# One layer on one core: the copy of the transposed probabilities is issued in front of the mask-and-maximum of a step

## The chip, the cores and the metric

The program runs on one core of one Trainium2 chip. The metric is the device time of one launch in microseconds (us), the median of three runs. The engines are called as in the profile: PE is TensorE (matmul; PEld its weight loads), DVE is VectorE, ACT is ScalarE, POOL is GpSimd, SP is SyncE.

## The reference, cut to what matters

Sizes: B=4, L=1024, D=256, 16 heads of 16, windows of 64 tokens; 8 experts, 2 per token, hidden size 1024.

```python
xn = layernorm(x)                                   # over D
# attention: each block of 64 queries sees its own 64 keys and the 64 before it
scores = einsum('bhnqd,bhnkd->bhnqk', qb, k_kv) * 0.25
scores = where(band_mask, scores, -1e30)
attn = softmax(scores, axis=-1)
ob = einsum('bhnqk,bhnkd->bhnqd', attn, v_kv)
# mixture of experts: top 2 of 8 with a capacity, relu(disp @ w1 + b1) @ w2 + b2, weighted by the gate
out = x + (ob, heads joined) @ w_out + moe(xn)
```

## The kernel before, in words

Four phases follow one another, each a block of its own: the norm, the routing, the experts (`moe_phase`), and the attention (`attention_phase`, line 788), which ends with the residual, the gathered outputs of the experts and the store. The change lies in the attention phase, which takes the span from about 461 us on.

The attention phase cuts the 4096 tokens into 8 units of 512 tokens (two to a batch element). A unit is 16 steps (`STEPS`), so there are 128 steps; a step `t` is one head pair's share of four tiles (`BLK` = 4) of 128 queries-by-keys, that is a tile of 128x512. For a step the engines do, each in its own loop over steps and with its own lag:

- PE writes the scores of two steps at a time (line 1212, at every even step, for steps t+2 and t+3). Before it does, it waits for the mask-and-maximum of all steps up to `t` (line 1205), because the bank of PSUM that holds the scores of step t+2 is the one of step `t`.
- DVE adds the mask to the scores, scales, writes them to SBUF and takes the row maximum, four instructions to a step (line 1088, "mask-and-maximum"); each releases ACT.
- ACT takes the exponential and its row sum (line 1059), four to a step.
- DVE takes the reciprocal of the sums of two steps at once (line 1096), at every even step, for steps t-2 and t-1, and releases POOL.
- POOL multiplies the probabilities by it (line 990, four to a step), and at every even step issues one gather of the experts' outputs (line 1000).
- PE transposes the probabilities of step t-4 (line 1226) into one of two banks of PSUM, `psP`; it first waits for POOL and for the copy of step t-6, which held that bank.
- DVE copies the transposed probabilities of step t-5 from `psP` to `pT` in SBUF (line 1103, "copy").
- Every fourth step PE multiplies them with the values (line 1246), and ACT and DVE bring the result out (lines 1041, 1130, 1046, 1135).

Between these PE works off the projections of the next unit and the output product of the last one in parts (lines 1170 and 1185, `psA`), which ACT and DVE read out (DVE lines 1070, 1075 and 1142). At every odd step DVE also adds one gathered tile of the experts' outputs to the residual (line 1122).

The order is written out by hand: each engine runs its program in order, and the steps of one engine follow each other as its `steps` function lists them. In a step DVE's list is: mask-and-maximum, reciprocal (even steps), copy, read-outs of `psA`, gathered tile (odd steps), and, every fourth step each, lines 1130 and 1135. `alone` is a wait that is an instruction of its own.

```python
LAG_T, LAG_C, LAG_V, LAG_O = 4, 5, 6, 7
...
pe.wait_ge(max_done, (b * BS + t - 1) * BLK)             # scores(b, t): masks of all steps before t-1
...
pe.wait_ge(pT_done[g % 2], b * STEPS + g // 2)           # transpose g: copy g-2
```

Of the kernel before, what the change touches and what calls it, by code (L numbers as in the profile page):

```python
# [40 lines left out]
def alone(eng, sem, value):  # L41


    eng.wait_ge(sem, value)
    eng.sem_inc(Mem.passed, 1)
# [742 lines left out]
def attention_phase(nc, m, x, xn_dram, y_dram, out):  # L788
# [11 lines left out]
    STEPS = NH // 2 * UB // BLK  # L800
    UNITS = B * 2

    LAG_T, LAG_C, LAG_V, LAG_O = 4, 5, 6, 7
# [20 lines left out]
    PR, PTR, YG = 8, 8, 4  # L824
    GRP = 4
    ctx = ExitStack()
    with ctx:
# [16 lines left out]
        pT = sb("a_pT", [P, PTR, BLK, P], fp32)  # L844
# [9 lines left out]
        psP = [ps("a_psP0"), ps("a_psP1")]  # L854
# [8 lines left out]
        t_done, pT_done = two("a_t_done"), two("a_pT_done")  # L863
        pv_done = sem("a_pv_done")
# [9 lines left out]
        BS, HB = 2 * STEPS, NI  # L874

        def count(b, u, i, first, last):

            n = NI * u + PRO - UT + i
            if first and u == 0 and i < O_FIRST:
                n += UT  # L880
            if last and u == 1:
                n -= O_FIRST
            return b * HB + n // 2
# [8 lines left out]
        def ended(t, first, last):  # L892

            if t is None or t >= BS:
                return []
            return [(i,) + there(t, i, first, last) for i in done_at[t % STEPS] if there(t, i, first, last)]

        def batches(eng, body, tail):

            body(0, True, False)  # L900
            for b in range(1, B - 1):
                body(b, False, False)
            body(B - 1, False, True)
            tail(B - 1)

        def lagged(t, lag, first):

            return None if first and t < lag else t - lag

        def group_out():  # L910

            return psO[:, :].rearrange("p (n s t) -> p n s t", n=BLK, s=2)

        def o_cols(parts, g):

            i = g // GRP % (STEPS // GRP)
            cols = slice((i % 2) * BLK * WIN, (i % 2 + 1) * BLK * WIN)
            return parts[g // STEPS % 2][:, i // 2, cols].rearrange("p (n t) -> p n t", n=BLK)
# [146 lines left out]
        @block.vector  # L1065
        def _(dve):
            def read_item(kind, j, u, n, bank, xh_count):
                if kind == "x":
                    dve.wait_ge(x_high, xh_count)
                    dve.tensor_tensor(xTl[:, j, :], psA[bank][:, :], xTh[:, j, :].bitcast(fp32), ALU.subtract)\  # L1070
                        .then_inc(item_free[bank], 1)
                elif kind == "k":

                    dve.wait_ge(item_done[bank], n + 1)
                    dve.tensor_copy(kT[u][:, j, WIN:WIN + UL], psA[bank][:, :]).then_inc(item_free[bank], 1)

            def steps(b, ts, first, last):
                for t in ts:
                    if t < BS:
                        r = t % PR  # L1080
                        if not (first and t < PR):

                            dve.wait_ge(t_done[t % 2], b * STEPS + (t - PR) // 2 + 1)
                        alone(dve, s_done, b * BS + t + 1)
                        for j in range(BLK):

                            band = 1 if t < STEPS and t // GRP % 2 == 0 and j == 0 else 0
                            dve.tensor_tensor_reduce(  # L1088
                                out=pr[:, r, j, :], in0=psS[bank_of[t % 4]][:, j * P:(j + 1) * P],
                                in1=m.mask[:, band, :], scale=-(DH ** -0.5), scalar=BIG,  # L1090
                                op0=ALU.add, op1=ALU.min, accum_out=nmax[:, r, j:j + 1]).then_inc(max_done, 1)
                    g = lagged(t, 1, first)
                    if g is not None and g < BS and g % 2 == 1:
                        pair = slice((g - 1) % PR, (g - 1) % PR + 2)
                        dve.wait_ge(exp_done, (b * BS + g + 1) * BLK)
                        dve.reciprocal(rsum[:, pair, :], sums[:, pair, :]).then_inc(rsum_done, 2)  # L1096
                    g = lagged(t, LAG_C, first)
                    if g is not None and g < BS:
                        dve.wait_ge(t_done[g % 2], b * STEPS + g // 2 + 1)
                        if not (first and g < PTR):  # L1100

                            dve.wait_ge(pv_done, b * (BS // GRP) + (g - PTR) // GRP + 1)
                        dve.tensor_copy(pT[:, g % PTR, :, :].rearrange("p c q -> p (c q)"), psP[g % 2][:, :])\  # L1103
                            .then_inc(pT_done[g % 2], 1)
                    for i, u, kind, j in ended(lagged(t, LAG_I, first), first, last):
                        n = count(b, u, i, first, last)
                        if kind == "o":
                            add_out((1 - u) % 2, j, n, i % 2, (b * 2 + u) * K * UT)
                        else:
                            read_item(kind, j, (1 - u) % 2, n, i % 2, (b * 2 + u + 1) * KD + j + 1)  # L1110
                    g = lagged(t, LAG_Y, first)
                    if g is not None and g < BS and g % 2 == 0:
                        u, i = g // STEPS % 2, g % STEPS // 2
                        ub = b * 2 + g // STEPS
                        tile, k = i // K, i % K
                        if i == 0:
                            dve.wait_ge(res_in[u], 16 * (b + (g // STEPS + 2) // 2))

                        dve.wait_ge(yg_in[i % YG], 16 * (ub * (K * UT // YG) + i // YG + 1))
                        if k == 1:  # L1120
                            dve.wait_ge(acc, ub * K * UT + i)
                        dve.scalar_tensor_tensor(res[u][:, tile, :], yg[i % YG][:, :],  # L1122
                                                 m.gates[:, bass.ds(ub * UT + k * NT + tile, 1)],
                                                 res[u][:, tile, :], ALU.mult, ALU.add).then_inc(acc, 1)
                    g = lagged(t, LAG_O, first)
                    if g is not None and g < BS and g % GRP == GRP - 1:

                        r = g // GRP % 2
                        dve.wait_ge(o_even, b * (BS // GRP) + g // GRP + 1)
                        dve.scalar_tensor_tensor(of[:, r, :, :], group_out()[:, :, 1, :], parity[:, 1:2],  # L1130
                                                 of[:, r, :, :], ALU.mult, ALU.add).then_inc(o_free, 1)
                    g = lagged(t, LAG_O + 1, first)
                    if g is not None and g % GRP == GRP - 1:
                        dve.wait_ge(o_high, b * (BS // GRP) + g // GRP + 1)
                        dve.tensor_tensor(o_cols(oTl, g), of[:, g // GRP % 2, :, :], o_cols(oTh, g).bitcast(fp32),  # L1135
                                          ALU.subtract).then_inc(o_low, 1)

            def add_out(u, j, n, bank, sums_before):

                dve.wait_ge(acc, sums_before)  # L1140
                dve.wait_ge(item_done[bank], n + 1)
                dve.tensor_tensor(res[u][:, j, :], res[u][:, j, :], psA[bank][:, 0:D], ALU.add)\  # L1142
                    .then_inc(item_free[bank], 1)

            def tail(b):
                steps(b, range(BS, BS + LAG_O + 1), False, True)
                for j in range(UT):
                    add_out(1, j, count(b, 1, NI - UT + j, False, True), j % 2, UNITS * K * UT)
            batches(dve, lambda b, first, last: steps(b, range(BS), first, last), tail)

        @block.tensor
# [181 lines left out]
```

## Time and profile before

| | |
|---|---|
| median of 3 runs | 759.27 us (757.99 to 761.73) |
| the profiled execution's own time | 760.58 us |
| its span | 758.8 us |
| DVE, ACT, POOL busy in the span | 63%, 63%, 56% |
| PE, PE weight loads busy in the span | 93%, 80% |

The span is what the engines' first and last instruction enclose; 1.8 us of the execution's own time lie around it. The shares are averages over four phases with different limits; the attention phase has to be read by itself. In the rows below `L1088` is line 1088 of the kernel, `out<-in` are the names of the tiles, and a bracket behind an instruction gives the time that its engine sat idle before it and what ended that.

### The profile page before, as it was taken

To read this page: it belongs to the slowest core of one execution; us is meant where nothing else is said; L and a number is where in the kernel's file an instruction comes from. 1 tells how busy PE (TensorE), PEld (TensorE's weight loads), DVE (VectorE), ACT (ScalarE), POOL (GpSimd) and SP (SyncE) were. 2 spreads that over 40 slices of the span, in tenths; PEclk is the share of its full clock that TensorE was granted. 3 is DMA by queue.
4 is the path that set the end of the run, shared out by engine and by line. 5 is a ranking of instruction groups with operands and counts; after the bars stand their busy time and mean duration, and the time that the engine had idled before them with its cause. 6 is when DMAs were issued, how large, how long until landed. Compare 5 with 4: busy or idle time off the path is not lost. (4 is left out here: it accounts for less than half of the span.)

```text
span 758.8 us, 18403 instructions
## 1 busy us (share of the span) xinstructions
PE 705.8 (93%) x5816; PEld 603.4 (80%) x5817; DVE 481.7 (63%) x1774; ACT 480.2 (63%) x1508; POOL 427.7 (56%) x818
## 2 busy tenths in 40 slices
PE   6686799999999999999999997999999999999885
PEld 3364689898898988989889896788888878878664
DVE  7773243543425345253452524999999989999994
ACT  4640480834709357192561905998989989999891
POOL 4502560543605336153351303899999989999993
PEclk8875699999999999999999998999999999999897
DMA  9722231142311423123241013132333415141411
GB/s 314 277 77 77 87 104 58 62 138 83 110 56 60 140 76 114 54 74 125 76 124 42 0 43 108 35 91 85 96 96 85 121 53 141 37 120 36 115 57 42
DMA packets 52308, 69.95 MB, mean 92 GB/s; under 512 B 6672, under 2 KB 44816, under 8 KB 52240
## 3 DMA queue, kind: packets, MB, share of 16 engines
q1 hardware_dynamic: 45744, 52.31, 21.3%
q0 software_dynamic: 6144, 16.79, 8.0%
q8 instruction: 32, 0.52, 0.3%
q14 instruction: 36, 0.29, 0.1%
q10 hardware_dynamic: 352, 0.04, 0.0%
HBM read 47.75 MB, written 16.78 MB: 85 GB/s over the span
## 5 line engine op out<-in xcount | busy, mean ns | idle before, releaser
L1059 ACT ACTIVATE a_p<-a_p,a_nmax 128x128 f32<-128x128 f32 x512 | 198.6, 395 | 35.6 <-DVE a_nmax L1088 35.4
L990 POOL TENSOR_SCALAR a_p<-a_p,a_rsum 128x128 f32<-128x128 f32 x512 | 192.3, 391 | 18.8 <-DVE a_rsum L1096 16.5
L719 DVE TENSOR_TENSOR m_hl<-m_hf,m_hh 128x512 fp32r<-128x512 f32 x128 | 93.1, 727 | 100.3 <-ACT m_hh L676 100.3
L55 PE MATMUL m_psY<-m_w2h,m_hh 128*128 128x256 f32 x512 | 145.1, 283 | 0.0
L55 PE MATMUL m_psY<-m_w2l,m_hh 128*128 128x256 f32 x512 | 143.8, 281 | 0.0
L55 PE MATMUL m_psY<-m_w2h,m_hl 128*128 128x256 f32 x512 | 143.8, 281 | 0.0
L672 ACT ACTIVATE m_hf<-m_psF,b1T 128x512 f32<-128x512 f32 x128 | 88.4, 691 | 66.3 <-PE m_psF L55 52.1
L640 POOL CAST m_w2h<-raw 128x256 fp32r<-128x256 f32 x64 | 25.4, 396 | 175.8 <-PE m_psY L55 120.5
L1088 DVE CUSTOM_DVE_ANT_0 a_p<-a_psS,mask 128x128 f32<-128x128 f32 x512 | 116.6, 281 | 6.3 <-PE a_psS L1212 5.1
L55 PE MATMUL m_psF<-m_xh,w1h 128*128 128x512 f32 x256 | 103.6, 405 | 1.9 <-DVE m_xl L696 1.9
L55 PE MATMUL m_psF<-m_xh,w1l 128*128 128x512 f32 x256 | 102.1, 399 | 0.0
L55 PE MATMUL m_psF<-m_xl,w1h 128*128 128x512 f32 x256 | 102.0, 398 | 0.0
L1059 ACT ACTIVATION_READ_ACCUMULATOR a_p<-a_p,a_nmax 128x1 f32 x512 | 99.5, 194 | 0.0
L705 DVE TENSOR_TENSOR y<-m_psY,b2b 128x256 f32<-128x256 f32 x64 | 27.2, 425 | 113.2 <-PE m_psY L55 113.2
L55 PEld LDWEIGHTS m_psY<-m_w2l,m_hh 128*128 128x128 f32 x512 | 96.5, 189 | 0.4
L55 PEld LDWEIGHTS m_psY<-m_w2h,m_hh 128*128 128x128 f32 x512 | 96.4, 188 | 0.4
L55 PEld LDWEIGHTS m_psY<-m_w2h,m_hl 128*128 128x128 f32 x512 | 96.5, 188 | 0.0
L660 ACT ACTIVATE m_xh<-m_psT 128x512 fp32r<-128x512 f32 x32 | 19.1, 600 | 113.9 <-PE m_psT L741 98.9
L1226 PE MATMUL a_psP<-eye,a_p 128*128 128x128 f32 x512 | 83.9, 288 | 5.2 <-DVE a_pT L1103 4.0
L676 ACT ACTIVATE m_hh<-m_psF,b1T 128x512 fp32r<-128x512 f32 x128 | 87.2, 681 | 0.0
L1103 DVE COPY a_pT<-a_psP 128x512 f32<-128x512 f32 x128 | 84.6, 661 | 1.7 <-PE a_psP L1226 1.4
L1226 PEld LDWEIGHTS a_psP<-eye,a_p 128*128 128x128 f32 x512 | 58.6, 145 | 20.5 <-POOL a_p L990 7.7
(186 smaller groups left out, 1363.1 us busy)
## 6 DMA issues: line engine op xcount, KB each, us to landing
raw<-in_L_ffn_w SPq DMA_DIRECT2D x16, 1024.0 KB, 5.3
y_scratch<-y SPq DMA_DIRECT2D x64, 128.0 KB, 1.7
n_xin<-in_L_attn_x SPq DMA_DIRECT2D x8, 512.0 KB, 7.4
xn_scratch<-n_xn SPq DMA_DIRECT2D x8, 512.0 KB, 7.6
a_res<-in_L_attn_x SPq DMA_DIRECT2D x8, 512.0 KB, 3.8
out<-a_res SPq DMA_DIRECT2D x8, 512.0 KB, 3.0
xnr<-xn_scratch SPq DMA_DIRECT2D x7, 512.0 KB, 5.1
b2b<-in_L_ffn_b SPq DMA_DIRECT2D x8, 128.0 KB, 4.8
```

What stands on the lines that cost most here:

```text
L55: last = pe.matmul(out, a, b, start=(n_start and i == 0), stop=(n_stop and i == n - 1))
L640: pool.tensor_copy(w2h[:, c, :], raw2[:, c, :]).then_inc(w2h_done, 1)
L660: act.activation(xh[:, g % KD, (g // KD) * HALF:(g // KD + 1) * HALF], psT[g % 2][:, :], ACT.Copy)\
L672: act.activation(hf[:, u % FR, :], psF[u % 4][:, :], ACT.Relu, bias=bias)
L676: act.activation(hh[:, u // HC, u % HC, :], psF[u % 4][:, :], ACT.Relu, bias=bias)\
L705: dve.tensor_tensor(yb[:, s % YR:s % YR + 1, :], psY[s % 2][:, 0:D].unsqueeze(1), m.b2b[:, bass.ds(e, 1), :], ALU.add).then_inc(yb_done, 1)
L719: dve.tensor_tensor(hl[:, u // HC, u % HC, :], hf[:, u % FR, :], hh[:, u // HC, u % HC, :].bitcast(fp32), ALU.subtract).then_inc(hl_done, 1)
L990: pool.tensor_scalar(e, e, rsum[:, r, j:j + 1], 0.0, ALU.mult, ALU.add).then_inc(norm_done, 1)
L1059: act.activation(e, e, ACT.Exp, scale=-1.0, bias=nmax[:, r, j:j + 1], accum_out=sums[:, r, j:j + 1]).then_inc(exp_done, 1)
L1088: dve.tensor_tensor_reduce(out=pr[:, r, j, :], in0=psS[bank_of[t % 4]][:, j * P:(j + 1) * P], in1=m.mask[:, band, :], scale=-(DH ** -0.5), ...
L1103: dve.tensor_copy(pT[:, g % PTR, :, :].rearrange("p c q -> p (c q)"), psP[g % 2][:, :])\
L1226: ins = pe.transpose(psP[g % 2][:, j * P:(j + 1) * P], pr[:, g % PR, j, :], m.eye[:, :])
```

## The change

DVE's list for a step begins with the copy of step t-5; the mask-and-maximum and the reciprocal follow it. The copy's two waits (for the transpose, and for the product that used the slot of `pT` before) move with it. Nothing else is edited: the same instructions, the same tiles, the same lags.

```diff
             def steps(b, ts, first, last):
                 for t in ts:
+                    g = lagged(t, LAG_C, first)
+                    if g is not None and g < BS:
+                        dve.wait_ge(t_done[g % 2], b * STEPS + g // 2 + 1)
+                        if not (first and g < PTR):
+
+                            dve.wait_ge(pv_done, b * (BS // GRP) + (g - PTR) // GRP + 1)
+                        dve.tensor_copy(pT[:, g % PTR, :, :].rearrange("p c q -> p (c q)"), psP[g % 2][:, :])\
+                            .then_inc(pT_done[g % 2], 1)
                     if t < BS:
                         r = t % PR
...
                         dve.reciprocal(rsum[:, pair, :], sums[:, pair, :]).then_inc(rsum_done, 2)
-                    g = lagged(t, LAG_C, first)
-                    if g is not None and g < BS:
-                        dve.wait_ge(t_done[g % 2], b * STEPS + g // 2 + 1)
-                        if not (first and g < PTR):
-
-                            dve.wait_ge(pv_done, b * (BS // GRP) + (g - PTR) // GRP + 1)
-                        dve.tensor_copy(pT[:, g % PTR, :, :].rearrange("p c q -> p (c q)"), psP[g % 2][:, :])\
-                            .then_inc(pT_done[g % 2], 1)
                     for i, u, kind, j in ended(lagged(t, LAG_I, first), first, last):
```

## Rows read from the trace of the kernel before

**Rows 1.** The busy line of the page: us, share of the span, instructions.

```profile
PE 705.8 (93%) x5816; PEld 603.4 (80%) x5817; DVE 481.7 (63%) x1774; ACT 480.2 (63%) x1508; POOL 427.7 (56%) x818
```

**Rows 2.** Two units by window: length, busy us by engine, PEclk, DMA share, GB/s.

```profile
600.70:637.50 36.80, 35.64 (x402) 29.73 (x401) 34.62 (x177) 32.51 (x147) 32.51 (x74) 0.95 0.30 77
672.10:706.70 34.60, 34.13 (x402) 28.67 (x401) 34.47 (x178) 32.56 (x147) 32.26 (x74) 1.00 0.29 79
```

**Rows 3.** Waits in the attention phase: us in total, times, longest.

```profile
POOL a_p L990 <- DVE a_rsum L1096: 16.5, 25, 6.8
PEld a_psS L1212 <- DVE a_nmax L1088: 15.9, 26, 1.6
...
PE a_psP L1226 <- DVE a_pT L1103: 4.0, 4, 1.2
...
DVE a_rsum L1096 <- ACT a_p L1059: 1.0, 3, 0.5
```

**Rows 4.** The chain that ended last, 664 to 700 us, by line.

```profile
by line: PE a_psA L1185 29.0%; PE a_psS L1212 24.4%; PE a_psP L1226 20.3%; PE a_psO L1246 11.2%; DVE a_p L1088 5.5%; PE a_psA L1170 3.0%; issue 2.1%; DVE a_pT L1103 1.7%; DVE a_res L1142 0.9%; DVE a_res L1122 0.8%; DVE a_oTl L1135 0.4%; DVE
```

**Rows 5.** Groups of instructions: busy us, mean ns; the last: ns min/median/max.

```profile
L990 POOL TENSOR_SCALAR a_p<-a_p,a_rsum 128x128 f32<-128x128 f32 x512 | 192.3, 391 | 18.8 <-DVE a_rsum L1096 16.5
L1088 DVE CUSTOM_DVE_ANT_0 a_p<-a_psS,mask 128x128 f32<-128x128 f32 x512 | 116.6, 281 | 6.3 <-PE a_psS L1212 5.1 <-issue 1.2
...
L1103 DVE COPY a_pT<-a_psP 128x512 f32<-128x512 f32 x128 | 84.6, 661 | 1.7 <-PE a_psP L1226 1.4 <-issue 0.2
...
L1122 DVE SCALAR_TENSOR_TENSOR a_res<-a_yg,gates,a_res 128x256 f32<-128x256 f32 x64 | 37.0, 577 | 1.8 <-DMA a_yg<-y_scratch,a_idx 1.8
...
L1122 DVE SCALAR_TENSOR_TENSOR a_res<-a_yg,gates,a_res x64: 466/574/743, 474.7 to 746.8; 128x256 f32<-128x256 f32 x64
```

**Rows 6.** PE in order of time, one unit: start, length, instruction.

```profile
664.97 1.16 PE L1212 MATMUL a_psS<-a_k,a_q 32*128 32x128 f32 x16 [0.60 <-DVE a_nmax L1088]
...
688.06 0.66 PE L1226 MATMUL a_psP<-eye,a_p 128*128 128x128 f32 x4
...
699.57 1.16 PE L1212 MATMUL a_psS<-k,q 32*128 32x128 f32 x16 [0.47 <-DVE a_nmax L1088]
```

**Rows 7.** DVE in order of time, the same unit.

```profile
687.63 0.68 DVE L1103 COPY a_pT<-a_psP 128x512 f32<-128x512 f32 x1
688.23 0.56 DVE L1122 SCALAR_TENSOR_TENSOR a_res<-a_yg,gates,a_res 128x256 f32<-128x256 f32 x1
...
689.05 0.28 DVE L1088 CUSTOM_DVE_ANT_0 a_p<-a_psS,mask 128x128 f32<-128x128 f32 x1
...
690.11 0.20 DVE L1096 RECIPROCAL a_rsum<-a_sums 128x8 f32<-128x8 f32 x1
...
698.59 0.28 DVE L1088 CUSTOM_DVE_ANT_0 a_p<-a_psS,mask 128x128 f32<-128x128 f32 x1
...
699.43 0.19 DVE L1096 RECIPROCAL a_rsum<-a_sums 128x8 f32<-128x8 f32 x1
```

**Rows 8.** DVE near the start of the phase.

```profile
472.90 0.69 DVE L1103 COPY a_pT<-a_psP 128x512 f32<-128x512 f32 x1 [0.87 <-PE a_psP L1226]
...
496.92 0.20 DVE L1096 RECIPROCAL a_rsum<-a_sums 128x8 f32<-128x8 f32 x1 [0.47 <-ACT a_p L1059]
```

**Rows 9.** POOL at the end of the phase.

```profile
733.95 1.41 POOL L990 TENSOR_SCALAR a_p<-a_p,a_rsum 128x128 f32<-128x128 f32 x4 [0.31 <-DVE a_rsum L1096]
...
744.84 1.41 POOL L990 TENSOR_SCALAR a_p<-a_p,a_rsum 128x128 f32<-128x128 f32 x4
```

**Rows 10.** A late gather in the long unit of Rows 2: DVE, then PE.

```profile
609.53 0.56 DVE L1122 SCALAR_TENSOR_TENSOR a_res<-a_yg,gates,a_res 128x256 f32<-128x256 f32 x1 [1.18 <-DMA a_yg<-y_scratch,a_idx]
...
611.33 1.16 PE L1212 MATMUL a_psS<-k,q 32*128 32x128 f32 x16 [1.16 <-DVE a_nmax L1088]
```

**Rows 11.** The two stretches with a low clock, by window (columns as in Rows 2).

```profile
613.00:617.00 4.00, 4.00 (x42) 3.12 (x41) 4.00 (x21) 3.15 (x15) 3.82 (x10) 0.57 0.14 35
715.76:721.00 5.24, 5.24 (x54) 4.20 (x55) 3.97 (x22) 2.72 (x15) 5.05 (x14) 0.50 0.10 28
```

## The prediction

> **What bounds the kernel now.** I read the page's busy line first [rows 1]: PE 93%, DVE, ACT and POOL near 60%. That is an average over four phases and says nothing of the attention phase, where alone the edit acts. So next the windows, one to a unit of 16 steps [rows 2]: a quiet unit takes 34.60 us, and DVE is busy for 34.47 of them, PE (by modelled ends) for 34.13, ACT 32.56, POOL 32.26. DVE has 0.1 us of idle time in a unit and POOL has 2.3. Third, the waits of the phase [rows 3]: PE's scores waited for the mask-and-maximum 26 times (15.9 us on the weight loads), PE's transposes for a copy only 4 times, 4.0 us, and POOL waited for a reciprocal 25 times. Fourth, the chain [rows 4]: in the unit at 664 to 700 us it is 88% PE (29.0 + 24.4 + 20.3 + 11.2 + 3.0), entered through a mask-and-maximum. Last, the order of time [rows 6, 7]: PE waits for DVE at 664.97 (0.60 us idle) and then not again until 699.57 (0.47). Together: DVE's list is full, and PE, 98% full, runs just behind it. What counts is not who gets work earlier but whether DVE, which never waits now, comes to wait.
>
> **The change part by part.**
>
> *Removed and added: nothing.* 128 copies of 661 ns and 512 mask instructions stay [rows 5]. Start to start a copy takes 0.60 (687.63 to 688.23), four mask instructions 0.84 (698.59 to 699.43) [rows 7]. In a step both stand next to each other before and after, so DVE's list is as long as before: 0. No DMA is issued by the moved copy, and none stands behind it in DVE's queue; POOL's gathers stand behind POOL's scalings, which hang on the reciprocal, and that one is now 0.60 later in its step (below).
>
> *What comes 0.60 earlier or later.* The copy itself starts 0.84 to 1.06 earlier; for PE's transposes, which wait for it seldom, this is worth at most the 4.0 us of [rows 3]. These 4 waits are near the start and the end, where POOL or the clock is late next; I take 0 for them. Mask-and-maximum and reciprocal end 0.60 later in their step, and with them PE's scores, ACT's exponentials and POOL's scalings. Behind the copy's wait now stand, on DVE, the masks, the reciprocal and everything else; PE, ACT and POOL wait for these.
>
> *Does DVE come to wait?* The copy of a step needs a transpose that PE ends one step before. Where the margin is smallest in the unit, the transpose starts at 688.06 and ends at 688.72, and the step that copies it starts at 689.05 with its masks [rows 6, 7]. Now the copy stands in that place: 0.33 us to spare. But PE's work moves as well. The scores at 664.97 had waited for the masks of their step; these end 0.60 later, and PE, with nothing to make it up until 699.57, carries the 0.60 along. 0.33 less 0.60: DVE waits some 0.3 there, once a unit. The loop that this closes can be added up. PE from the scores to the end of the transpose: 688.72 - 664.97 = 23.75. Handover to DVE, taken as long as the one from DVE to PE (699.43 to 699.57): 0.14. Four steps of DVE, 698.59 - 689.05 = 9.54; in them the reciprocal at 690.11 stood 0.21 behind the end of its masks (689.05 + 0.84 = 689.90), a small wait for ACT that the copy, now in front, covers: 9.33. Then the copy and the masks of the next step that PE waits for, 0.60 + 0.84, and the handover 0.14: 1.58. Sum 23.75 + 0.14 + 9.33 + 1.58 = 34.80, against 34.60 from scores to scores before. So +0.20 a unit, and with five such intervals +1.0. Bounds: 0, if PE makes up the 0.60 somewhere; +2.0, if the 0.21 isn't covered. The other transposes of the unit have more room, and POOL's 2.3 us of idle time a unit take up its later start.
>
> *Reciprocals that wait for ACT.* 1.0 us in 3 waits [rows 3], the longest 0.47 at 496.92 [rows 8]. The copy, 0.60, now runs in front of it, under the wait. Gain 0.45 there; the other two lie where a new wait for the transpose takes their place. -0.45 (bounds -1.0 and 0).
>
> *Start of the phase.* The first copy waited 0.87 for its transpose, behind its masks [rows 8]. Now the masks (0.84) are behind the wait. The next steps are PE's at that point, which hides most of it: +0.3 (bounds 0 and +0.84).
>
> *End of the phase.* From 733.95, where it waited 0.31 for a reciprocal, POOL goes on without a wait for DVE to its last scaling at 744.84 + 1.41 = 746.25 [rows 9], and the last product hangs on that. This reciprocal is 0.60 later: +0.6. Before it lies a stretch with a granted clock of 0.50, 715.76 to 721.00 [rows 11], in which transposes take longer and the copy's wait would hold up the masks: +0.3 (bounds 0 and +1.9, about the copy, the masks and the transpose in series).
>
> *The gathered tile* (line 1122) takes 466 to 743 ns, 577 in the mean [rows 5], by what POOL does at the time. Its place in DVE's list stays, but POOL moves by up to 0.60 against it. All 64 at their shortest would give 64 x (0.577 - 0.466) = -7.1; all at their longest +10.6. They are a mix of both now and I expect another mix: 0, with 2 us either way in the range.
> The Trainium skill (GPSIMD Engine Reference, Specifications) says that GpSimd shares its SBUF interfaces with VectorE and that they contend when a DVE instruction has two SBUF inputs. Line 1122 has two, the copy has none (its input is in PSUM); by that rule only a change of phase matters, the order of copy and masks by itself doesn't, and the spread of 466 to 743 ns agrees with it.
>
> **Sum:** -0.45 + 0.3 + 1.0 + 0.9 = +1.75 us. The profiled execution took 760.58 (span 758.8, 1.8 around it), so 762.3 for one like it. That execution was 1.3 above the median of the runs, 759.27; on the median I predict 761.0.
>
> **The rivals.**
>
> *A, the other side: the clock of PE falls at the longer wait.* In the long unit of [rows 2] a late gather held DVE for 1.18 and PE for 1.16 us [rows 10]; from 613 to 617 the granted clock was 0.57 [rows 11], half rate for most of it. That unit took 36.80, 2.2 more than a quiet one, so about 1.0 went to the clock. With the change the wait of 0.60 at 664.97 becomes up to 1.20, as long as the one at 611.33. If that alone decides, each of the six quiet units of this kind loses 1.0 to 2.2 on top: 9 us, 770. It decides from a wait of about 1.1 us in front of the scores. For it: the same place, the same length. Against: the longer wait comes once; by the loop above PE's idle time then settles near 0.8 (34.80 less the 34.0 of PE's own work), and 0.60 has cost no clock so far.
>
> *B, faster: DVE's gathered tiles get out of POOL's way, and the waits of transposes for copies go.* Half of 7.1, and half of 4.0: -5.5, 753.8. For it: both exist in the rows. Against: the rows of line 1122 show no place where all would be helped, and where transposes wait for copies, something else is late too.
>
> *C, nothing: DVE's list has the same length and the margins hold.* 759.3. For it: 34.47 of 34.60 is DVE. Against: 0.33 is less than 0.60.
>
> *D, slower through DVE: the margins fail at every even step.* Each of the 50 or so rounds of quiet units would lose some 0.2 to 0.3: +12, 771. It would need PE later than the rows show it by another 0.5 us.
>
> **How the numbers follow.** What a measurement of this kernel can tell from no change is about 0.5%, 3.8 us, so 755.5 to 763.1 is "no change". Forecast 0.45 and C 0.20 both lie in it: 0.65. A 0.14 and D 0.08: slower 0.22. B 0.13: faster. The likeliest one's own range is 758.5 to 764, from the bounds of its terms. The range for 8 in 10 takes in C, a part of B and the cheap end of A: 756 to 766.
>
> **What the profile after would show.** Right: units of 34.6 to 34.9 us with DVE still over 34.3 busy; the copy waiting for its transpose some 0.1 to 0.4 us once a unit, at the ninth step; scores waiting 0.7 to 1.2 for the masks in front of the 13th step, in fewer places; no reciprocal waiting for ACT at 497; the last scaling of POOL about 1 us nearer the end of a longer span. Wrong: a PEclk below 1.00 in the quiet units (A); copies waiting in many steps (D); a mean of line 1122 far from 577 ns (B, or its opposite); a unit of 34.4 or less, which would mean that PE's loop was the bound and not DVE's list.

## The result, and the profile after

| | before | changed |
|---|---|---|
| median (range), 16 runs each, same chip | 760.16 us (757.99 to 763.94) | 764.77 us (761.70 to 767.23) |
| ratio to before, 95% interval | | 1.005 (1.0037 to 1.0063) |
| profiled execution, its span | 760.58, 758.8 | 764.19, 762.4 |

The kernel became slower by 0.5%, 3.8 us by the ratio (the medians differ by 4.6). I had predicted 761.0, +1.75. The time lies in the range of 756 to 766; the loss is twice what I made it. Its interval, 0.37 to 0.63%, excludes no change, while 0.65 of my chances lay on a time up to 763.1 that I had called no change. The sum was made of other terms than the trace shows.

The page's busy line and two windows: a unit, over the length from the masks of one 13th step to the next, then the end of the phase (columns as in [rows 2]).

```profile
PE 705.1 (92%) x5816; PEld 602.8 (79%) x5817; DVE 482.1 (63%) x1774; ACT 481.7 (63%) x1508; POOL 423.2 (56%) x818
```

```profile
673.10:708.40 35.30, 34.13 (x399) 28.30 (x397) 34.46 (x177) 32.88 (x147) 31.39 (x74) 1.00 0.28 79
740.00:760.00 20.00, 13.20 (x104) 10.66 (x104) 7.97 (x17) 2.32 (x8) 6.43 (x15) 0.57 0.05 15
```

The busy line is nearly the same as in [rows 1] (POOL 423.2 for 427.7); the loss is in the windows. A quiet unit took 34.60 us with DVE busy for 34.47 [rows 2]. It now takes 35.30 with DVE busy for 34.46: the work is the same, and 0.7 us of idle time and of slower issue have come in. PE's granted clock is 1.00, its upper level, so the clock has no part in it. The waits of the phase (us in total, times, longest):

```profile
ACT a_p L1059 <- DVE a_nmax L1096: 40.0, 33, 24.8
...
PE a_psS L1212 <- DVE a_nmax L1096: 11.8, 26, 1.1
...
DVE a_pT L1085 <- PE a_psP L1226: 3.8, 8, 1.7
...
DVE a_xTl L1070 <- issue: 2.4, 5, 0.5
...
DVE a_xTl L1070 <- ACT a_xTh L1017: 1.2, 2, 0.7
```

Read them against [rows 3]. The reciprocal's wait for ACT (1.0 us, 3 times) is gone, as forecast. The copy waits for its transpose, 8 times, three of them at the 9th step of a unit: forecast too. But six waits of 0.49 us (one 0.48) stand in front of line 1070, the subtraction that makes the low half of the next unit's x, where there were none (the 0.7 that is left in the ACT row is at the start of the phase, as before). In the first of the six the profile names ACT's read-out of x as the releaser; in the other five it says "issue", which names none, and the order of time does. ACT, then DVE, then PE, in the unit of [rows 6, 7]:

```profile
664.70 0.40 ACT L1059 ACTIVATE a_p<-a_p,a_nmax 128x128 f32<-128x128 f32 x1 [0.93 <-DVE a_nmax L1096]
...
669.06 0.38 ACT L1024 ACTIVATE va<-a_psA 128x256 f32<-128x256 f32 x1 [0.40 <-PE a_psA L1185]
...
674.80 1.06 ACT L1017 ACTIVATE a_xTh<-a_psA 128x512 fp32r<-128x512 f32 x2
```

```profile
664.39 0.27 DVE L1096 CUSTOM_DVE_ANT_0 a_p<-a_psS,mask 128x128 f32<-128x128 f32 x1
...
674.63 0.29 DVE L1096 CUSTOM_DVE_ANT_0 a_p<-a_psS,mask 128x128 f32<-128x128 f32 x1
...
675.41 1.29 DVE L1070 TENSOR_TENSOR a_xTl<-a_psA,a_xTh 128x512 fp32r<-128x512 f32 x2 [0.49 <-issue]
...
689.91 0.69 DVE L1085 COPY a_pT<-a_psP 128x512 f32<-128x512 f32 x1 [0.29 <-PE a_psP L1226]
...
699.08 0.68 DVE L1085 COPY a_pT<-a_psP 128x512 f32<-128x512 f32 x1
699.68 0.27 DVE L1096 CUSTOM_DVE_ANT_0 a_p<-a_psS,mask 128x128 f32<-128x128 f32 x1
```

```profile
665.36 1.16 PE L1212 MATMUL a_psS<-a_k,a_q 32*128 32x128 f32 x16 [0.40 <-DVE a_nmax L1096]
...
678.62 1.16 PE L1212 MATMUL a_psS<-k,q 32*128 32x128 f32 x16 [0.34 <-DVE a_nmax L1096]
...
682.97 1.16 PE L1212 MATMUL a_psS<-k,q 32*128 32x128 f32 x16 [0.31 <-DVE a_nmax L1096]
```

PE's scores now wait for masks at three places of a unit, the 13th, the 3rd and the 5th step; in a quiet unit before it was the 13th alone. In the phase that makes 26 such waits of PE, 11.8 us, for 12 of 7.6 us before.

And the place in the kernel before that I had not read, ACT and then DVE:

```profile
664.32 0.40 ACT L1059 ACTIVATE a_p<-a_p,a_nmax 128x128 f32<-128x128 f32 x1 [0.91 <-DVE a_nmax L1088]
...
674.41 1.06 ACT L1017 ACTIVATE a_xTh<-a_psA 128x512 fp32r<-128x512 f32 x2
```

```profile
674.40 0.68 DVE L1103 COPY a_pT<-a_psP 128x512 f32<-128x512 f32 x1
675.02 1.29 DVE L1070 TENSOR_TENSOR a_xTl<-a_psA,a_xTh 128x512 fp32r<-128x512 f32 x2
```

This is a loop through three engines. The masks of the 13th step release ACT, which then runs four steps of exponentials and its read-outs with one more gap of 0.40, up to the read-out of x (line 1017); 0.61 after that starts, DVE can subtract (line 1070); from there DVE's own list leads to the masks of the next 13th step. From masks to x the loop takes 675.02 - 664.00 = 11.02 before, 675.41 - 664.39 = 11.02 after. The other part is DVE's list: 698.59 - 675.02 = 23.57 before ([rows 7] has the 698.59), 699.68 - 675.41 = 24.27 after. Before, DVE came to line 1070 from a copy issued at 674.40, 0.62 earlier, and a copy holds it for 0.60: it arrived as x did, 0.02 ahead of it. The change takes that copy (0.60) out of the part that ACT covers, and puts one (699.08) between x and the next 13th-step masks, the part that DVE alone has to run. No instruction is added, but one of 16 copies has changed sides of a loop without slack. The 0.70 of the second part is that 0.60, with the copy's wait of 0.29 at the 9th step (689.91) added and the reciprocal's 0.21 of [rows 7] taken off, to within 0.02.

The chain over 664 to 700 us, by line, now runs through DVE and through waits without a releaser ("issue"):

```profile
by line: DVE a_p L1096 23.8%; issue 18.0%; PE a_psS L1212 9.5%; PE a_psA L1185 8.2%; PE a_psP L1226 7.4%; DVE a_pT L1085 7.0%; PE a_psO L1246 5.6%; DVE a_oTl L1135 4.0%; DVE a_res L1122 4.0%; DVE a_xTl L1070 3.2%; DVE a_nmax L1096 2.6%; DVE
```

It was 88% PE before [rows 4]. Neither chain is "the" bound: DVE and x came to line 1070 within 0.02 us of each other before, and a chain follows whichever came last.

Groups of the phase, as in [rows 5]:

```profile
L1085 DVE COPY a_pT<-a_psP 128x512 f32<-128x512 f32 x128 | 86.5, 676 | 4.6 <-PE a_psP L1226 3.8
...
L1122 DVE SCALAR_TENSOR_TENSOR a_res<-a_yg,gates,a_res 128x256 f32<-128x256 f32 x64 | 33.4, 522 | 1.8 <-DMA a_yg<-y_scratch,a_idx 1.7
...
L1135 DVE TENSOR_TENSOR a_oTl<-a_o,a_oTh 128x256 fp32r<-128x256 f32 x32 | 15.5, 484 | 0.5 <-ACT a_oTh L1046 0.5
...
L1130 DVE SCALAR_TENSOR_TENSOR a_o<-a_psO,parity,a_o 128x256 f32<-128x256 f32 x32 | 14.2, 443 | 5.1 <-ACT a_o L1041 5.1
```

Line 1122 lost 3.6 us (mean 577 to 522 ns), as the faster rival wanted, but line 1135 rose from 13.2 to 15.5 and the copies from 84.6 to 86.5. With line 1130 (15.1 to 14.2) the four make -3.6 + 2.3 + 1.9 - 0.9 = -0.3.

### The profile page after: what moved, and what is told of

It is laid out like the page before. It is cut to its first block and busy times, and to the rows that moved or that the text cites. A ratio compares the mean times of both kernels' runs of the same rounds, so it can differ in the third digit from the quotient of the medians.

```text
span 762.4 us, 18403 instructions
## 1 busy us (share of the span) xinstructions
PE 705.1 (92%) x5816; PEld 602.8 (79%) x5817; DVE 482.1 (63%) x1774; ACT 481.7 (63%) x1508; POOL 423.2 (56%) x818
## 5 line engine op out<-in xcount | busy, mean ns | idle before, releaser
L990 POOL TENSOR_SCALAR a_p<-a_p,a_rsum 128x128 f32<-128x128 f32 x512 | 185.5, 380 | 25.4 <-DVE a_rsum L1104 23.5
L1059 ACT ACTIVATION_READ_ACCUMULATOR a_p<-a_p,a_nmax 128x1 f32 x512 | 96.8, 189 | 0.0
L1085 DVE COPY a_pT<-a_psP 128x512 f32<-128x512 f32 x128 | 86.5, 676 | 4.6 <-PE a_psP L1226 3.8
```

The costliest lines, as they stand in the source:

```text
L990: pool.tensor_scalar(e, e, rsum[:, r, j:j + 1], 0.0, ALU.mult, ALU.add).then_inc(norm_done, 1)
L1059: act.activation(e, e, ACT.Exp, scale=-1.0, bias=nmax[:, r, j:j + 1], accum_out=sums[:, r, j:j + 1]).then_inc(exp_done, 1)
```

## The experiments

The first four ran on one chip, the next four on a second, the last three on a third; each is compared with the kernel before on its own chip. "Unit" is the time between the masks of two 13th steps, units in which a gathered tile came 0.25 us late or more left aside, and the first and last unit too (before: 34.6, one 34.90 behind a late unit; changed: 35.3, one 35.63).

| experiment | median | before there | ratio (95%) | unit |
|---|---|---|---|---|
| front at 13th step only | 775.52 | 768.84 | 1.0070 (1.0040, 1.0100) | 35.26 to 35.30 |
| all but the 13th | 771.15 | 768.84 | 1.0023 (1.0003, 1.0044) | 34.70 to 35.11 |
| all but 13th and 14th | 772.10 | 768.84 | 1.0037 (1.0017, 1.0057) | 34.73 to 34.91 |
| masks, copy, reciprocal | 771.93 | 768.84 | 1.0030 (1.0014, 1.0045) | 34.94 to 35.13 |
| changed, less ACT work | 772.09 | 768.79 | 1.0033 (1.0013, 1.0053) | 34.84 to 35.15 |
| changed, less PE work | 772.93 | 768.79 | 1.0047 (1.0023, 1.0071) | 35.03 to 35.23 |
| changed, less of both | 769.19 | 768.79 | 1.0022 (0.9997, 1.0046) | 34.64, 34.66 |
| before, less of both | 765.49 | 768.79 | 0.9957 (0.9940, 0.9974) | 34.56 |
| front at 9th step only | 755.64 | 761.44 | 0.9934 (0.9914, 0.9954) | 34.23 to 34.25 |
| changed, again | 764.26 | 761.44 | 1.0038 (1.0016, 1.0060) | 35.03 to 35.38 |
| before, again | 759.63 | 761.44 | 0.9977 (0.9945, 1.0008) | 34.58, 34.59 |

**One copy moved, the others as before.**

```diff
+                def front(t):
+                    return t < BS and t % STEPS == 12
...
+                    if front(t):
+                        copy(t)
                     ...masks, reciprocal...
+                    if not front(t):
+                        copy(t)
```

> The copy stands in front of the masks only at the 13th step of each unit (t mod 16 = 12), in all other steps behind them as in the kernel before: 8 of 128 copies are moved. Theory ACT (a loop of masks of the 13th step, ACT's exponentials and its read-out of x, VectorE's subtraction of x, and VectorE's list up to the next 13th step had no slack, and the one copy in front of these masks lengthens it by 0.6 us): the quiet unit goes to 35.1 to 35.3 us as with the whole change, VectorE waits 0.4 to 0.6 us in front of the subtraction (line 1070) in every unit, total +3 to +4 us against before. Theory PE (my prediction: the loop over PE's scores and the transpose copied in the 9th step): 34.6 to 34.8, total 0 to +1. Theory each step pays: one sixteenth of the effect, total +0.3.

Eight moved copies of 128 gave the whole unit cost: 35.26 to 35.30, and a ratio no smaller than the change's. A window and DVE's waits in it:

```profile
568.06:603.34 35.28, 34.13 (x400) 28.67 (x400) 34.55 (x178) 32.36 (x146) 32.40 (x74) 1.00 0.33 93
```

```profile
576.88 0.20 DVE L1109 RECIPROCAL a_rsum<-a_sums 128x8 f32<-128x8 f32 x1 [0.48 <-ACT a_p L1059]
...
578.42 0.69 DVE L1084 COPY a_pT<-a_psP 128x512 f32<-128x512 f32 x1
579.09 1.29 DVE L1070 TENSOR_TENSOR a_xTl<-a_psA,a_xTh 128x512 fp32r<-128x512 f32 x2
```

Masks (568.06) to x (579.09) is 11.03 again, and x to the next masks 24.25. The idle time shows two steps ahead of x, in front of a reciprocal that waits for the same ACT. Where a loop is tied, the place of the wait says little; the loop's length does. The late scores of PE start at the same masks, but in the four quiet units DVE waited for ACT alone (0.43 to 0.48 at this reciprocal, and 0.15 or 0.16 at line 1130's place in two of them) and nowhere for PE. So with this one copy moved the cost comes through ACT. The next experiments ask whether that is also the whole cost when all copies are moved.

**That copy left behind its masks, all others in front.** `front(t)` is true for every step but the 13th.

> The whole change except at the 13th step of each unit, where the masks go first as before. Theory ACT: the masks of the 14th step had no slack before ACT either (in the kernel before its first exponential starts 0.04 us after its mask), so a copy in front of them holds the loop just as well: unit 35.1 to 35.3, the wait in front of line 1070 stays at 0.4 to 0.6, while the copy's wait for its transpose at the 9th step (0.3) goes; total +3 to +4. Theory PE: PE's scores after the 13th step are no longer late, unit 34.5 to 34.6, total 0 to +1.

The wait in front of line 1070 is gone in the quiet units. I had expected it to stay, for want of room at the 14th step; of that only 0.25 is left (masks to x 11.26 to 11.28 in four of the five units, for 11.02). Units went to 34.70 to 35.11, 35.04 at the median, not 34.6: the wait of the copy at the 9th step rose from 0.29 to about 0.5 in four of the five.

```profile
579.34 1.29 DVE L1070 TENSOR_TENSOR a_xTl<-a_psA,a_xTh 128x512 fp32r<-128x512 f32 x2
...
593.84 0.69 DVE L1084 COPY a_pT<-a_psP 128x512 f32<-128x512 f32 x1 [0.49 <-PE a_psP L1233]
```

I had expected that wait to go with the late scores of the 13th step. It didn't: scores of the 1st, 3rd and 5th steps now start 0.97 to 1.01 after their masks began, the distance at which masks release them, where they started 1.57, 1.19 and 1.10 after them before. PE gets its lateness at other even steps too, and not by carrying it from the 13th.

**The same, with the 14th step's copy behind its masks as well.**

> The whole change except at the 13th and 14th step of each unit. Theory ACT: the loop is as short as before; no wait in front of line 1070, unit 34.3 to 34.6, total -1 to +1 against before (what is left is the start and the end of the phase). Theory PE: the same as without the 13th step alone, 34.5 to 34.6, so this run is told from the one before by the wait at line 1070. Theory each step pays: fourteen sixteenths of the effect, total +3 to +4.

Masks to x is 11.08, nearly the old length, in all quiet units but one (11.28), so the copy of the 14th step accounts for most of the 0.25. But the copy's wait at the 9th step stays at 0.5, and the quiet units are 34.73, 34.91 and 34.91 (a fourth, 35.24, has a gathered tile 0.25 late). I had expected 34.3 to 34.6. By the times the two experiments can't be told apart.

**Masks, then copy, then reciprocal**, so that the masks keep their place and only copy and reciprocal change sides.

```diff
                     ...masks...
+                    copy(t)
                     ...reciprocal (even steps)...
-                    ...copy...
```

> Order in a step: masks, copy, reciprocal. The masks are where they were before; the reciprocal is as late as in the whole change. Theory ACT: masks and exponentials run as before, no wait at line 1070; the reciprocals that waited for ACT (0.2 a unit, 0.5 at the 17th step) are covered: unit 34.4 to 34.6, total -2 to 0, with 0.6 given back at the end of the phase. Rival theory POOL (the effect comes from the later reciprocal, over POOL's scalings): as slow as the whole change, +3 to +4.

I expected 34.4 to 34.6 and no wait at line 1070; it was 34.94 to 35.13, with a wait of 0.40 to 0.47 there in every unit, put down to ACT in five of six. The part from masks to x grew from 11.02 to 11.5, and that is the 0.4 to 0.5 of the unit. ACT's order of time shows where it grew: a gap of 0.98 in front of the read-out of a product (line 1041), where there was none. DVE, PE and ACT in this experiment, in a unit whose 13th-step masks start at 602.37; then PE and ACT in the kernel before:

```profile
613.87 1.29 DVE L1070 TENSOR_TENSOR a_xTl<-a_psA,a_xTh 128x512 fp32r<-128x512 f32 x2 [0.47 <-ACT a_xTh L1017]
...
605.70 0.40 PE L1247 MATMUL a_psO<-a_pT,a_va 128*32 128x128 f32 x8
...
607.16 0.47 ACT L1041 ACTIVATE a_o<-a_psO,parity 128x256 f32<-128x256 f32 x1 [0.98 <-PE a_psO L1247]
```

```profile
667.33 0.40 PE L1246 MATMUL a_psO<-a_pT,a_va 128*32 128x128 f32 x8
...
667.80 0.48 ACT L1041 ACTIVATE a_o<-a_psO,parity 128x256 f32<-128x256 f32 x1
```

The profile puts the gap down to the product, but the product isn't late: its last instructions start 3.33 after the masks in both kernels (605.70 - 602.37, 667.33 - 664.00). ACT's read-out follows them 0.47 later before and 1.46 later here. So a copy in front of the reciprocal costs by itself, through ACT, though no mask moved; by what path it reaches ACT is not shown.

**Slack put into each loop of the changed kernel.** Line 1058 is cut for three steps a unit (the exponentials of the 15th, 16th and 1st step over 16 of 128 columns), which shortens ACT's part from masks to x. In another, the products of the low half of the query weights are left out, which shortens PE's part. A third has both, and a control is the kernel before with both.

```diff
-                            e = pr[:, r, j, :]
+                            e = pr[:, r, j, slice(56, 72) if t % STEPS in (14, 15, 0) else slice(0, P)]
...
+                    if kind == "q" and low_l:
+                        continue
```

> The kernel after, with ACT's exponentials of the 15th, 16th and 1st step of each unit taken over 16 of the 128 columns (the others are left as scores; the output is not the reference's). That takes some 0.1 us from each of 12 instructions, about 1 us, out of ACT's part of the loop from the masks of the 13th step to ACT's read-out of x, and leaves VectorE's and PE's lists as they are. Theory ACT: VectorE's wait of 0.49 in front of line 1070 goes, the copy's wait of 0.3 at the 9th step stays, the quiet unit falls from 35.3 to 34.8. Theory PE (the scores that wait for later masks are what costs, and the wait at line 1070 is only a sign of it): unit stays at 35.3.

> The kernel after, with the two products of the low half of the query weights left out on PE (q is less exact; two of them, 0.46 us, lie between the scores of the 5th step and the transpose that the copy of the 9th step waits for). Theory ACT with the copy's wait in series: the copy's wait of 0.3 at the 9th step goes, the 0.49 in front of line 1070 stays, unit 35.0. Theory PE alone: unit 34.5 to 34.7.

> The kernel after with both shortenings. Both waits go: unit 34.4 to 34.6, as in the control, if the two waits are the whole of the cost in a unit. If a unit stays 0.2 or more above the control, the rest is in VectorE's list itself (longer gathered-tile and low-half instructions beside POOL).

> Control: the kernel before with both shortenings, ACT's exponentials as in the run before this one and, on PE, the two products of the low half of the query weights left out (0.23 us each, for four of the 24 q and k products of a unit). VectorE's list was the bound of the unit; both theories: 34.3 to 34.6, at most the 0.2 of the reciprocal that waited for ACT is gained.

Windows of the four in this order, with two of the third:

```profile
567.15:602.18 35.03, 33.76 (x400) 28.46 (x399) 34.28 (x178) 31.62 (x146) 31.12 (x73) 1.00 0.31 92
```

```profile
531.10:566.33 35.23, 33.37 (x398) 27.93 (x396) 34.35 (x178) 32.57 (x146) 31.22 (x74) 1.00 0.32 94
```

```profile
564.52:599.55 35.03, 33.15 (x398) 27.91 (x396) 34.10 (x178) 31.79 (x146) 31.62 (x74) 1.00 0.31 93
599.55:634.19 34.64, 33.10 (x397) 27.92 (x396) 34.10 (x177) 31.71 (x146) 31.41 (x74) 1.00 0.33 96
```

```profile
598.85:633.41 34.56, 33.42 (x398) 27.85 (x398) 34.29 (x178) 31.80 (x146) 32.21 (x74) 1.00 0.32 96
```

With ACT shortened the wait in front of line 1070 is gone (masks to x 10.45), but the copy waits 0.46 to 0.50 in its place. With PE shortened it is the other way: the copy's wait is gone, x waits 0.49 as before, and a reciprocal waits for ACT:

```profile
542.13 1.29 DVE L1070 TENSOR_TENSOR a_xTl<-a_psA,a_xTh 128x512 fp32r<-128x512 f32 x2 [0.49 <-issue]
...
558.03 0.20 DVE L1104 RECIPROCAL a_rsum<-a_sums 128x8 f32<-128x8 f32 x1 [0.34 <-ACT a_p L1059]
```

Only with both does a unit come back to 34.64, within 0.1 of the control. The units in between, 35.03 and 35.00, have a wait at a gathered tile, at the same place of the unit; the profile puts one down to the gather and names nothing for the other (line 1122 in the unit of 35.03, of 34.64, of 35.00):

```profile
580.47 0.53 DVE L1122 SCALAR_TENSOR_TENSOR a_res<-a_yg,gates,a_res 128x256 f32<-128x256 f32 x1 [0.47 <-issue]
...
615.16 0.49 DVE L1122 SCALAR_TENSOR_TENSOR a_res<-a_yg,gates,a_res 128x256 f32<-128x256 f32 x1
...
650.00 0.66 DVE L1122 SCALAR_TENSOR_TENSOR a_res<-a_yg,gates,a_res 128x256 f32<-128x256 f32 x1 [0.34 <-DMA a_yg<-y_scratch,a_idx]
```

So with slack in both loops almost the whole cost of a quiet unit goes: 35.3, about 35.0 with the one, 35.2 with the other, 34.65 with both. The control gained 0.4% of time though its units are the old 34.56, so its gain lies outside them: before the change DVE's list alone holds a unit at 34.6, and slack on ACT and PE is of no use in it.

**The copy in front at the 9th step only.** The 9th step lies in the part of the loop that DVE runs alone, and there the reciprocal stood 0.21 behind its masks for ACT [rows 7]. A copy in front covers that, and it stays in the same part of the loop, since both its places lie there.

```diff
-                    return t < BS and t % STEPS == 12
+                    return t < BS and t % STEPS == 8
```

> The copy stands in front of the masks only at the 9th step of a unit, where in the kernel before the reciprocal stood about 0.21 us behind its masks for ACT; everywhere else as before. Loop-through-ACT theory: the part of the loop from the masks of the 13th step to the x subtraction stays 11.02, the other part loses the 0.21 (and gets at most a copy's wait of 0.1 in its place), so quiet units of 34.4 to 34.5 instead of 34.6, about -0.2 x 5 = -1 us, a ratio of 0.998 to 1.000, which these rounds can hardly tell from 1. Rival, that any copy in front of masks costs DVE by itself: one of 16 copies moved would cost 0.7 / 16 = 0.04 a unit and the 0.21 would not go, 34.6 to 34.7. Second rival, the sum of my prediction (the copy waits for its transpose once the scores carry 0.60): that needs the late scores of the 13th step, which are not moved here, so it says no copy wait and 34.4 as well; a copy wait of 0.3 or more at this step would speak against it.

```profile
659.32:693.57 34.25, 34.13 (x403) 28.69 (x402) 34.25 (x178) 32.43 (x146) 32.09 (x74) 1.00 0.28 81
```

```profile
684.43 0.68 DVE L1084 COPY a_pT<-a_psP 128x512 f32<-128x512 f32 x1
685.03 0.27 DVE L1101 CUSTOM_DVE_ANT_0 a_p<-a_psS,mask 128x128 f32<-128x128 f32 x1
...
685.88 0.19 DVE L1109 RECIPROCAL a_rsum<-a_sums 128x8 f32<-128x8 f32 x1
```

No wait at the reciprocal (0.85 behind the first mask, where it was 1.06) and none at the copy. Masks to x is 11.06, x to masks falls from 23.57 to 23.19. This is the loop's arithmetic in the other direction: a unit of 34.25. Of the 0.38, 0.21 is the reciprocal's wait, as expected; the other 0.16 was not forecast: the next two gathered tiles held DVE for 0.45 and 0.46, where they had held it for 0.52 and 0.55. DVE is busy for all of the unit. It is also faster than both kernels, 0.9934 (0.9914 to 0.9954), 5.0 us. That is more than I expected (about 1). Of the 5.0 the trace shows 2.6 between the first masks of the phase and those of the last step: 271.40 us against 273.99 in the repeat of the kernel before (start -0.3; first unit +0.5 with a gather 1.0 late; four units of -0.35; -0.6 in one whose gather was less late; -0.8 in the last). The rest I can't assign: it would need many profiles, since late gathers come in some executions and not in others.

**Both kernels once more.**

> The changed kernel once more, unedited, on the chip of this call. Loop-through-ACT theory: quiet units of 35.3 again, waits of 0.49 in front of the x subtraction in every unit, the 9th-step copy waiting about 0.3; ratio 1.003 to 1.007. For the end of the phase: if the low clock there (20.4 us from the last masks to the end, against 17.0 in the kernel before) belongs to the changed order, it comes again; if it is a matter of the execution, this profile may show anything from 17 to 20.5. Rival, that the extra 0.7 a unit was a matter of the one profiled execution: units between 34.6 and 35.3 this time.

> The kernel before once more, unedited. Ratio 1.000. Quiet units of 34.6 (the one with a late gather aside), no wait in front of the x subtraction past the first unit. For the end of the phase: if the high clock of the final products (3.24 us for the last group) belongs to this order, the time from the last masks to the end is 17.0 again; if it is a matter of the execution, it may be up to 20.5.

The units repeat: 35.03 to 35.38 with a wait of 0.49 in front of line 1070 in each of the six units that have one; 34.58 and 34.59 with none. From the first masks of the phase to those of the last step it was 273.99 and 278.86 us, 4.9 apart (276.03 and 277.35, 1.3 apart, in the first two profiles, with the late gather of [rows 10] in the shorter). The ratio, 1.0038, agrees with the first one within the intervals.

## Why the prediction was right or wrong, point by point

- **What bounds.** "DVE's list is full, and PE runs just behind it" held: DVE is busy for 34.46 of 35.30, and in the 9th-step version for all of 34.25. I looked for slack between DVE and PE only. ACT, at 32.56 of 34.60, looked free; but in the stretch from the 13th-step masks to the x read-out it has two gaps (0.91 and 0.40), and DVE's arrival there had 0.02 to spare. A mean over a unit hid a tied loop.
- **The failed step: "+0.20 a unit".** The sum from scores to scores gave 34.80, and it left ACT out: the loop through ACT gives 11.02 + 24.27 = 35.3, which is +0.7. The repeat and the 13th-step experiment (whole effect from one copy, DVE waiting for ACT alone) show it, and the 9th-step version shortens the same loop by what it says. With all copies in front it is not the only one: take the x wait away and a unit stays near 35.0, held by the copy; slack in both brings 34.65.
- **The copy's wait, forecast 0.3: the number right by luck.** It was 0.29 to 0.31 in the three units that had one (0.19 to 0.34 in the repeat). But I had PE carry 0.60 from the scores at 664.97 to the transpose with nothing to wait for, 23.75. In the changed kernel that stretch is 689.88 - 665.36 = 24.52, and 0.65 of the 0.77 more are the two new waits for masks, 0.34 and 0.31: PE's lateness at the transpose comes from the masks of the 5th step. The experiment that left the 13th step's copy behind shows the same, as the copy's wait grew there instead of going.
- **Five intervals.** Measured 0.7 each, 3.5 where I had 1.0. Six intervals hold an x read-out; in the repeats the six together took 211.63 against 208.44, 3.2 more, with a late gather in the shorter.
- **Reciprocals, -0.45.** The wait at 497 went, and 0.49 in front of line 1070 at 498 took its place: 0.
- **Start, +0.3.** From the first masks to the 13th-step masks 25.79 went to 26.10; 27.08 in the repeat. Right for one profile, 1.0 short for the other.
- **End, +0.9.** POOL's last scaling ended 7.91 after the last step's masks, then 8.34 (8.31 in the repeat): +0.4 for 0.6. The clock part was of another kind than I thought (below).
- **Gathered tile, 0.** The sum held, for a reason I had only half: line 1122 gained, and lines 1135 and 1103 lost. My expectation on the mean of 577 ns was wrong (522). Two of the shifts go with the place behind the reciprocal, which the copy gave up at most even steps and line 1130 took at most of its own: copies took 15 ns more and line 1130 took 29 ns less in the mean (see the last section). The runs bear on the rule of the Trainium skill that I had cited (GPSIMD Engine Reference, Specifications: contention when a DVE instruction has two SBUF inputs) as far as that lines 1122 and 1135, which have two, moved most, by -55 and +70 ns in the mean (-63 and +37 in the repeats). No run took POOL's work away to test it.
- **Rivals.** A, a falling clock: no, PEclk 1.00 in the units. PE's wait in front of the 13th step's scores was 0.75 once and then 0.40, where I foretold 0.7 to 1.2, and such waits came in more places, not in fewer. In the experiment with one copy moved it was 1.14 to 1.24, past the 1.1 at which A was to decide, and PEclk was 1.00 in the quiet units there as well. B: its mechanism came, its gain was given back. Line 1122 lost 3.6 us, half of the 7.1; PE's transposes no longer wait for a copy, but wait 5.1 us for POOL where it was 1.1, and their idle time is 5.2 us in both kernels. C, nothing: the list did stay as long (34.46), the margins didn't hold. D, DVE waiting at every even step: no, at two places a unit.

Added up: 3.5 in the units, 0.3 at the start, 0.4 at the end, 4.2, against 3.8 by the ratio. That they agree is weak support: in the two pairs of profiles the stretch from the first masks of the phase to the last step's grew by 1.3 and by 4.9. And that the time fell into the range owes something to its width, made for other rivals: 764.77 is above the 764 that I gave the likeliest case.

## What to carry to other kernels

When an engine's list is full, moving an instruction within it is not free of charge because the list stays as long: cut the list at each point where another engine's result has to be there, and add up each piece with its loop. A piece that another engine covers may lose work and gain nothing by it; the other piece pays. Then look for the place where the engine already waits inside the piece that it runs alone, and move work in front of that wait only: here one copy of 16 gave -0.7%, all 16 gave +0.5%. Read the time from loop start to loop start; where the wait appears in a tied loop says little.

## What the runs showed of the hardware that was not expected

The last product of the phase ran at two clocks, whatever the order of the copies. Its first instruction on PE and the window over its 24, in the kernel before and in its repeat:

```profile
751.53 0.36 PE L1185 MATMUL a_psA<-wout_h,a_oTh 128*128 128x256 f32 x1 [2.11 <-DVE a_oTl L1135]
...
751.50:754.80 3.30, 3.24 (x24) 2.99 (x24) 1.26 (x3) 0.00 (x0) 0.00 (x0) 1.00 0.00 0
```

```profile
750.97 0.55 PE L1185 MATMUL a_psA<-wout_h,a_oTh 128*128 128x256 f32 x1 [2.10 <-DVE a_oTl L1135]
...
750.97:756.44 5.47, 5.45 (x24) 5.16 (x24) 1.26 (x3) 0.00 (x0) 0.00 (x0) 0.50 0.00 0
```

The same program, the same wait of 2.1 us in front, nearly the same granted clock from the last step's masks up to it (0.74 and 0.73): the upper level and 3.24 us for the 24 products in one, the lower and 5.45 in the other. From the last step's masks to the end it was 16.96 and 20.70 us (20.42 and 19.14 in the two profiles of the changed kernel). So 3.5 of the 3.6 us between the two profiled executions that I had to compare lie in this end. The units' loss did not show in that total: a late gather had cost the profile of before 2.2 us, and its phase started 1.2 us later. Two profiles with the right difference in total can have it in the wrong places. What decides the clock at the end stays open.

Two smaller ones. A copy most often holds DVE for 0.56 us behind a reciprocal and for 0.60 behind anything else. This doesn't belong to the copy: with the copy moved away, what stands behind the reciprocal has the 0.04 instead (line 1142 0.29 for 0.33, line 1075 0.56 for 0.60), so the move costs nothing by it. And line 1135, 128x256 with two inputs in SBUF, took 421 ns at the median and up to 634 ns in the changed kernel, where it had been 412 and at most 426. That the order of copy and masks shifts a collision with POOL's work from line 1122 to line 1135 would fit both; it is not shown.
